# Rotating queries and keys in the layout they are multiplied in, without turning them first

## The reference

```python
qkv = x @ w_qkv (+ bias in the first attention)
q: 32 heads of 16, k and v: 8 heads of 16
rot = concatenate([-x2, x1])           # x1, x2: the two halves of a head
q, k = q * cos + rot * sin, k * cos + rot * sin   # cos, sin depend on the token
scores = softmax(q @ k.T * scale, masked to keys <= query)
out = (scores @ v) @ w_dense
```

## Time and profile before

| | us |
|---|---|
| median of 3 runs (lowest, highest) | 2409.13 (2407.0, 2411.66) |
| profiled execution: its time, its span | 2416.49, 2414.8 |
| PE busy (share of the span) | 2254.6 (93%) |
| VectorE busy | 1464.6 (61%) |
| ScalarE busy | 1183.2 (49%) |
| GpSimd busy | 506.3 (21%) |
| mean granted clock of TensorE | 0.963 |

### The profile page before, as it was taken

The page is one execution under the profiler, slowest core; times in us unless marked ns, Lnnn a source line. Parts: engine busy times, 40 slices in busy tenths (PEclk is TensorE's granted clock), DMA queues, the critical chain, the costliest instruction groups (busy, mean ns, idle before and its releaser), DMA issues.

```text
span 2414.8 us, 36047 instructions
## 1 busy us (share of the span) xinstructions
PE 2254.6 (93%) x12664; PEld 1220.6 (51%) x12664; DVE 1464.6 (61%) x3257; ACT 1183.2 (49%) x2273; POOL 506.3 (21%) x646
## 2 busy tenths in 40 slices
PE   6688898999999999999899999989898999999998
PEld 5455554545455455555555555545443444444443
DVE  6767787857667576787877778777752221221222
ACT  5465677645556465565666666576861101011010
POOL 4433323212312122131312222122220000000000
PEclk8699898999999999999999999999999999999999
DMA  5000324312313123231413133243323000000000
GB/s 179 1 1 19 104 82 164 103 47 72 117 42 114 35 58 120 80 108 53 144 53 112 54 106 116 78 122 98 100 61 97 0 18 0 14 5 5 13 1 18
DMA packets 135122, 163.59 MB, mean 68 GB/s; under 512 B 41616, under 2 KB 96912, under 8 KB 134672
## 3 DMA queue, kind: packets, MB, share of 16 engines
q1 hardware_dynamic: 134944, 161.29, 21.7%
HBM read 94.51 MB, written 53.35 MB: 61 GB/s over the span
## 4 chain that ended last, share of the span: by engine, by line
PE 76%; DMA 6%; DVE 6%; ACT 4%; SPq 3%; issue 2%; POOL 1%; ACTq 0%; POOLq 0%; DVEq 0%
PE ps L1505 15%; PE ps L1443 10%; PE ps L1516 7%; PE ps L1413 7%; PE ps L1397 7%; PE ps L1422 5%; PE ps L1458 5%; PE ps L1367 3%; PE ps L1286 3%; DMA scr_q<-big 3%; PE ps L1372 3%; PE ps L1467 2%; PE ps L1490 2%; PE ps L1378 1%; DVE peaks L2086 1%
## 5 line engine op out<-in xcount | busy, mean ns | idle before, releaser
L2086 DVE TENSOR_REDUCE peaks<-ps 128x4 f32<-128x512 f32 x960 | 625.0, 681 | 220.3 <-PE ps L1367 91.3
L1697 ACT ACTIVATE big<-ps 128x512 f32<-128x512 f32 x960 | 551.5, 603 | 362.7 <-PE ps L1397 252.9
L1901 POOL TENSOR_SCALAR_AFFINE_SELECT big<-big 128x512 f32<-128x512 f32 x384 | 248.3, 660 | 1010.6 <-ACT big L1697 1010.2
L1505 PE MATMUL ps<-xt,big 128*128 128x512 f32 x896 | 390.1, 593 | 2.8 <-issue 2.8
L1397 PE MATMUL ps<-big 99*128 99x512 bf16 (+3 forms) x1536 | 347.5, 305 | 23.5 <-ACT big L1697 18.2
L1443 PE MATMUL ps<-big,xt 128*128 128x512 f32 (+1 forms) x768 | 295.7, 497 | 0.5 <-DVE peaks L2086 0.2
L1505 PEld LDWEIGHTS ps<-xt,big 128*128 128x128 f32 x896 | 168.8, 190 | 209.3 <-issue 208.2
L1413 PE MATMUL ps<-big,vs 128*32 128x512 f32 (+3 forms) x3072 | 247.7, 450 | 11.5 <-POOL big L1901 8.2
L1786 ACT ACTIVATE t<-ps 128x512 f32<-128x512 f32 x56 | 33.5, 598 | 457.6 <-PE ps L1505 457.6
L1686 ACT ACTIVATE ps<-cbf 128x512 f32<-128x512 bf16 x384 | 230.8, 605 | 37.3 <-DVE peaks L2086 31.5
L2142 DVE SCALAR_TENSOR_TENSOR t<-rest,t 128x512 f32<-128x512 f32 x56 | 38.7, 691 | 280.4 <-PE ps L1505 276.8
(11 more groups left out here) (225 smaller groups left out, 2906.2 us busy)
## 6 DMA issues: line engine op xcount, KB each, us to landing
big<-scr_q SPq DMA_DIRECT2D x96, 384.0 KB, 4.1
scr_q<-big SPq DMA_DIRECT2D x48, 384.0 KB, 2.9
scr_q<-big SPq DMA_DIRECT2D x48, 256.0 KB, 3.1
recb<-scr_sums SPq DMA_DIRECT2D x96, 128.0 KB
big<-scr_k SPq DMA_DIRECT2D x48, 192.0 KB, 3.3
big<-in_ffn_gu SPq DMA_DIRECT2D x14, 512.0 KB, 6.2
scr_q<-big SPq DMA_DIRECT2D x48, 128.0 KB, 3.2
ctxt<-ots SPq DMA_DIRECT2D x192, 32.0 KB
```

What stands on the lines that cost most here:

```text
L1505: mm = pe.matmul(bank_of(kind, n, m), wgu[:, m // 2, c, way, m % 2 * P:(m % 2 + 1) * P], xt[:, c, :], start=(c == 0), stop=(c == DC - 1))
L1697: act.activation(probs[:, i * S:(i + 1) * S], bank_of("exp", g, i), ACT.Exp, scale=1.0 / 16 if attn_of(n) == 1 else 0.25).then_inc(made["p ...
L1901: pool.affine_select(block_, block_, [[0, GQ], [1, P]], ALU.is_ge, zero, base=0, channel_multiplier=-1).then_inc(made["cut"], 1)
L2086: dve.tensor_reduce(to, blocks, AX.X, ALU.max, negate=True).then_inc(made["negmax"], 1)
```

## The change

The projection of queries and keys is made with the weights as the stationary operand, so that a bank holds 128 columns of the projection by 512 tokens: chunk `c` of round `n`, in four matmuls of 512 columns. ScalarE copies the two halves of the bank crosswise into `r` (`swap`; the bias is added there in attention 1), VectorE multiplies the bank by the cosines into `t1` (`cosines`), and `rotate` multiplies `r` by signed sines and adds `t1`. `first_part` and `first_rest` read `r` in place of a bank, and there is no `turn_chunk`. The values have a unit of their own (`vproj`): sixteen matmuls of 128 columns into one bank, moved to `vs` by one instruction. The tables of cosines and sines must lie with columns of the projection on partitions, so PE turns `ropet` (`turn_tables`, item `tabs`) and ScalarE copies it out in four instructions (`rotations`), for attention 1 and, from a second load, for attention 2 and 3. All chunks of round n+1 now stand in the list ahead of the dense product of round n-1, where they stood among its blocks. The bias of queries and keys arrives as a 128x5 tile by an added, non-contiguous load. `t1`, `t2`, `a`, `r` and the bias tiles get smaller. Waits on `chunk_full` elsewhere become waits on `rest`. The diff, cut to its core:

```diff
-FRONT = ("inx", "inh", "th", "hm", "f", "hd")
+FRONT = ("tabs", "inx", "inh", "th", "hm", "f", "hd")
...
@@ -101,12 +101,10 @@
     if after < NIT:
         first += prepared(after)
     if before >= 0:
-        first = first[:-len(CHUNKS)] if after < NIT else []
-        rest = [[(0.45, ("chunk", after, c))] for c in CHUNKS] if after < NIT else [[]] * len(CHUNKS)
         for j in range(TJ):
             first += [(0.86, ("dense", before, j, c)) for c in range(DC)]
-            first += [(0, ("y", "d", before, j))] + rest[j]
-        first += [(0, ("ln", "d", before))] + rest[TJ]
+            first += [(0, ("y", "d", before, j))]
+        first += [(0, ("ln", "d", before))]
     spread(14 if n == NIT - 1 else 1, 46, first)
     if n == 0:
         spread(50, 66, [(0.5, item) for item in four_bit(2)])
...
+    items += [("tabs", 1), ("load_rope", 2)]
...
@@ -160,16 +159,11 @@
 
 def prepared(n):
     items = [(0.45, ("xt", "a", n, c)) for c in range(DC)]
-    late = []
-    for j in range(TJ):
-        for half in range(2):
-            for c in range(DC):
-                items.append((0.86 if half == 0 else 0.43, ("proj", n, j, half, c)))
-                if late and c % 2:
-                    items.append((0, late.pop(0)))
-            items.append((0, ("fill", n, j, half)))
-        late = [("rope", n, j, 0), ("rope", n, j, 1)]
-    return items + [(0, i) for i in late] + [(0.45, ("chunk", n, c)) for c in CHUNKS]
+    for nth, c in enumerate(CHUNKS):
+        if nth == 2:
+            items += [(0.9, ("vproj", n, j)) for j in range(TJ)] + [(0, ("vals", n))]
+        items += [(0.86, ("proj", n, c, k)) for k in range(DC)] + [(0, ("chunk", n, c))]
+    return items
 
 
...
         return [("PE", kind, k, columns(512, 1.68))]
     if kind == "proj":
-        return [("PE", kind, k, columns((512, 256)[k[2]], 1.68))]
+        return [("PE", "proj", k, columns(512, 1.68))]
+    if kind == "vproj":
+        return [("PE", "vproj", k, 920)]
+    if kind == "tabs":
+        return [("PE", "tabs", k, TURN), ("ACT", "rotations", k, 2500)]
...
-        return [("DVE", "added", k, 730) if attn_of(k[0]) == 1 else ("ACT", "filled", k, 660)]
-    if kind == "rope":
-        return [("DVE", ("turned", "rope")[k[2]], k[:2], (1900, 1050)[k[2]])]
+    if kind == "vals":
+        return [("DVE", "vadded", k, 750) if attn_of(k[0]) == 1 else ("ACT", "vfilled", k, 660)]
     if kind == "chunk":
-        return [("PE", "chunk", k, TURN), ("ACT", "hi", k, ROWS_ACT), ("DVE", "rest", k, ROWS_DVE),
+        return [("ACT", "swap", k, 1250), ("DVE", "cosine", k, 730), ("DVE", "rope", k, 1450), ("ACT", "hi", k, ROWS_ACT), ("DVE", "rest", k, ROWS_DVE),
                 ("ACT", "mid", k, 660), ("POOL", "lo", k, 1250), ("SP", "cw", k, 2000)]
...
+    if name == "tabs":
+        return [("load_rope", k)]
+    if name == "rotations":
+        return [("tabs_full", k)] + ([("rope", (NB - 1, CHUNKS[-1]))] if n == 2 else [])
...
+        late = [("y_full", ("f", n - 3, TJ - 1))] if k[1] == CHUNKS[1] and n >= 3 and attn_of(n - 3) < 3 else []
+        return [("proj_full", k)] + ([("rest", (n - 1, k[1]))] if n else []) + late
+    if name == "cosine":
+        before = chunk_before(n, k[1])
+        return [("proj_full", k), ("swap", k), ("rotations", (min(attn_of(n), 2),)), ("rope", before) if before else ("begin", ())]
     if name == "rope":
-        late = []
...
-        return [("rope", (NB - 1, TJ - 1))]
+        return [("tabs_full", (1,))]
...
-        if kind == "rope" and item[1:] == (3, TJ - 1, 1):
-            plan.append(("load_rope", 2))
+        if kind == "chunk" and item[1:] == (3, CHUNKS[-1]):
+            plan.append(("tabs", 2))
...
-        a = sb("a", [P, QK], F32)
-        t1 = sb("t1", [P, QK], F32)
-        t2 = sb("t2", [P, QK], F32)
-        r = sb("r", [P, TJ, QK], F32)
-        flat_r = r[:].rearrange("p j n -> p (j n)")
...
+                 (bias_v[:], ins["attn1_bqkv"][:, QK:QKV].broadcast_to((P, P))))
+            sp.dma_start(bias_c[:], ins["attn1_bqkv"][:, 0:QK].rearrange("o (c p) -> p (o c)", p=P),
+                         allow_slow_non_contiguous=True).then_inc(weights["attn1"], 16)
             sp.dma_start(t1[:, 0:3 * P], ins["masks"]).then_inc(constants, 16)
             flow_loads()
...
-                               start=(c == 0), stop=(c == DC - 1))
-                if c == DC - 1:
+                    bank_for("proj", n, c)
+                mm = pe.matmul(bank_of("proj", n, c), wp[:, k, c * P:(c + 1) * P], xt[:, k, :], start=(k == 0), stop=(k == DC - 1))
+                if k == DC - 1:
                     mm.then_inc(made["proj_full"], 1)
 
-            def turn_chunk(n, c):
-                pe.wait_ge(made["rope"], counted("rope", n, TJ - 1))
-                bank = bank_for("chunk", n, c)
-                turn_tiles(bank, lambda j: r[:, j, c * P:(c + 1) * P]).then_inc(made["chunk_full"], 1)
+            def project_values(n, j):
+                if j == 0:
+                    pe.wait_ge(made["xt"], counted("xt", "a", n, DC - 1))
+                    pe.wait_ge(proj_in, 16 * attn_of(n))
+                    bank_for("vproj", n)
+                for k in range(DC):
+                    mm = pe.matmul(bank_of("vproj", n)[:, j * P:(j + 1) * P], xt[:, k, j * P:(j + 1) * P], wp[:, k, QK:QKV],
+                                   start=(j == 0 and k == 0), stop=(k == DC - 1), skip_group_check=True)
+                if j == TJ - 1:
+                    mm.then_inc(made["vproj_full"], 1)
+            def turn_tables(A):
+                pe.wait_ge(rope_in, 16 * A)
+                bank = bank_for("tabs", A)
+                turn_tiles(bank, lambda j: ropet[:, j].rearrange("p w k -> p (w k)")).then_inc(made["tabs_full"], 1)
...
+            def rotations(A):
+                act.wait_ge(made["tabs_full"], counted("tabs_full", A))
+                if A == 2:
+                    act.wait_ge(made["rope"], counted("rope", NB - 1, CHUNKS[-1]))
+                bank = bank_of("tabs", A)
+                act.activation(cs[0:64, 0, :], bank[0:64], ACT.Copy)
+                act.activation(cs[64:P, 0, :], bank[0:64], ACT.Copy)
+                act.activation(cs[0:64, 1, :], bank[64:P], ACT.Copy, scale=-1.0)
+                act.activation(cs[64:P, 1, :], bank[64:P], ACT.Copy).then_inc(made["rotations"], 1)
+            def swap(n, c):
+                act.wait_ge(made["proj_full"], counted("proj_full", n, c))
+                if n:
+                    act.wait_ge(made["rest"], counted("rest", n - 1, c))
+                if c == CHUNKS[1] and n >= 3 and attn_of(n - 3) < 3:
+                    act.wait_ge(made["y_full"], counted("y_full", "f", n - 3, TJ - 1))
+                if n == 0 and c == CHUNKS[0]:
+                    act.wait_ge(weights["attn1"], 48)
+                bank = bank_of("proj", n, c)
+                if attn_of(n) == 1:
+                    act.activation(r[0:64, c, :], bank[64:P], ACT.Identity, bias=bias_c[64:P, c:c + 1])
+                    act.activation(r[64:P, c, :], bank[0:64], ACT.Identity, bias=bias_c[0:64, c:c + 1]).then_inc(made["swap"], 1)
                     return
-                if j == 0:
-                    act.wait_ge(made["pv_full"], counted("pv_full", 8 * (n - 2) + 7, 1))
-                act.activation(a[:, 512:QK], bank[:, 0:P], ACT.Copy)
-                act.activation(vs[:, n % 2, j, :, 0:HD], bank[:, P:2 * P].rearrange("p (h d) -> p h d", h=NKV),
-                               ACT.Copy).then_inc(made["filled"], 1)
...
                 slot = flow.slot[n, c]
-                act.wait_ge(made["chunk_full"], counted("chunk_full", n, c))
+                act.wait_ge(made["rope"], counted("rope", n, c))
                 if flow.written_by[n, c] > 1:
                     act.wait_ge(parts_out[slot], 48 * (flow.written_by[n, c] - 1))
-                act.activation(qp[:, slot, 0, :], bank_of("chunk", n, c), ACT.Copy).then_inc(made["hi"], 1)
+                act.activation(qp[:, slot, 0, :], r[:, c, :], ACT.Copy).then_inc(made["hi"], 1)
 
             def second_part(n, c):
...
+            def cosines(n, c):
+                dve.wait_ge(made["proj_full"], counted("proj_full", n, c))
+                dve.wait_ge(made["swap"], counted("swap", n, c))
+                dve.wait_ge(made["rotations"], counted("rotations", min(attn_of(n), 2)))
+                before = chunk_before(n, c)
+                if before:
+                    dve.wait_ge(made["rope"], counted("rope", *before))
                 else:
                     dve.wait_ge(made["begin"], counted("begin"))
-                dve.wait_ge(rope_in, 16 if attn_of(n) == 1 else 32)
-                cos = ropet[:, j, 0, :].unsqueeze(1).broadcast_to((P, 2 * CH, 64))
-                sin = ropet[:, j, 1, :].unsqueeze(1).broadcast_to((P, CH, 64))
-                ah = a[:].rearrange("p (c w k) -> p c w k", w=2, k=64)
-                th = t2[:].rearrange("p (c w k) -> p c w k", w=2, k=64)
```

(60 more changed lines are left out.)

135 lines of the change are left out of this document (56 added, 79 removed).

## The result

The changed kernel took 2425.98 us, the median of four runs (2423.69 to 2428.36), against 2408.65 us (2407.0 to 2411.66) for the kernel before beside it. The ratio is 1.0071 with a 95% interval of [1.0053, 1.0088]: 17.3 us slower. The forecast was 2415 (2387 to 2438), 6 us slower: the sign and the largest cause were right, and the result lies inside the range, but the change cost nearly three times what was forecast.

What follows compares the result with a forecast made beforehand. PE was taken as the bound from about 400 us, the chain from x's load before. -24.2 + 1.5 + 3 + 36 + 6 - 10 - 6 = +6.3 gave 2422.8 us profiled, 2415 in the median, range 2387 to 2438.

Steps and rivals of the forecast that it cites:

- Tables first in PE's order: At the start, PE waits for both tables and turns x at about 44 us, not 7.99: +36 us (30 to 40).
- One bank less: The second table holds its PSUM bank until round 3's last chunk, about 620 us: +6 us (0 to 26).
- Turned chunks: In rounds 1 to 11, PE no longer turns 55 chunks of r at 0.44 us each: -24.2 us.
- ScalarE and the longer path: ScalarE gets 40 us more work and chunks cross between ScalarE and VectorE six times: +3 us (-4 to +10).
- VectorE: Per round it loses some 11.4 us and gets 10.2, three operations a chunk at about 0.68 us each.
- Start and burst: Earlier first maxima, some 25 us after the first projection: -10 us; round 1's chunks one by one, not bursting: -6.
- values: The values' matmuls become short, 32 passes of 128 columns a round: +1.5 us (0 to 2.7).
- The signs of error: Wrong if x turns at 8 us, first exponents make up over 35 us, or rounds 1 to 8 don't shorten.
- A: The forecast itself, all terms as summed: 2415 us, own range 2403 to 2427; chance 0.50.
- D: The held bank and the chunks' longer way cost much more, 26 + 10: 2442 us, half-way 2430; chance 0.18.
- B: Early keys fill all PE loses at the start (20), the burst goes (14), bank only 2: 2393 us; chance 0.24.
- C: The tables don't stop PE, as x stands ahead or the table lands early: 2375 us; chance 0.08.

Runs made afterwards that it cites:

- the square: Four medians against before: upper row, first table early: second early +17.3, second late +2.8; lower row, first late: -14.0 and -28.6 us.
- E5: The kernel before with one added wait, so that PE doesn't start until the rotation table is in: 2440.19 us, ratio 1.0129.
- E2: The changed kernel with the first table modelled as landing at 60 us, so PE turns x first; second table's bank still held: 2392.37 us, ratio 0.9943.
- E3: The changed kernel with the first table modelled at 60 us and the second turned only after round 3's last chunk: 2377.79 us, ratio 0.9876.
- E6: The kernel before with each chunk of r turned twice into the same bank, 240 more transposes: 2430.28 us, ratio 1.0098.
- E10: E3 with one ScalarE copy of 128 partitions a chunk in place of two of 64, halves not swapped; second timing: 2374.45 us, ratio 0.9845.
- E11: E3 with two more ScalarE copies of 64 partitions in each chunk, four in all: 2404.49 us, ratio 0.9981.
- E9: The same kernel as E3, timed again: 2374.63 us, ratio 0.9857 to the kernel before.
- E4: E3 with the first table's modelled landing at 45 us in place of 60: 2374.1 us, ratio 0.9872.

## Why the prediction was right in sign and short in size

Along the square the 17.3 us are -28.6 for the change without the tables, +31.4 for the first table, +4 for the second one's load (x at 42.9 against 38.9) and +10.5 for what is left of the second; that they add up is by construction. The forecast had -35.7, +36 and +6. Its first two nearly cancel, so the sign that it gave hung on the 6 us of the bank alone: it was right by a margin smaller than the error of single terms. By its steps:

- **Tables first in PE's order** (+36): right. The order came out as forecast, and the first table landed at 38.1 us against 37.9; the second took 2.6 us to land, not 4.0, so x came at 42.85 against "about 44", and the first projection at 245 against "about 243". Measured were 31.4 and 4, and 33.8 for 30.8 in E5. One reading was wrong without consequence: the 3.66 us of sixteen transposes at the start were put to "the lower clock", but the trace gives a granted clock of 1.00 for 8 to 12 us (last section).
- **One bank less** (+6, up to 26): the term that was sized too low. "I take 6" stands against 10.5 us in the square's upper row and 14.6 in the lower. The interval of either row alone reaches down to about 5 us and so doesn't exclude the 6; that both rows lie above it, and that PE's waits grow alike in both, speaks for more. The bounds held. The one row of before that the step could name was that the trace "shows no wait put down to it", which speaks for nothing: as E2 beside E3 shows, a missing bank appears as waits on other engines. The place was right in part: its upper bound came from 250 to 300 us, and the traces of E2 and E3 part by 7.9 us before 207 us and by the rest between 207 and 420 us.
- **Turned chunks** (-24.2): right. E6 gives 0.42 us a chunk, and rounds 3 to 11 together are 23.9 us shorter than before's, 2.7 each, and 20.3 shorter than E5's, 2.3 each, against "some 2.2". Round by round that is uneven: round 3 gained 5.5 us (147.4 to 141.9), round 4 nothing (145.0 to 145.2).
- **ScalarE and the longer path** (+3, -4 to +10): not contradicted. The second copy is worth between 0 and 8 us by two timings. The upper end for one copy was right: 64 partitions by 512 took 684 ns with a bias and 128 partitions 687 (E10). ScalarE's busy time rose by 58.6 us in all, not 40. `first_part`, which now reads SBUF, took 626 ns on average against 600 from a bank, close to the 33 ns more that the prediction took from its rows. How near the load is to a limit is open: E11 says only that two copies more are too many.
- **VectorE**: the guess of 0.68 us an operation holds for the cosine product (0.69 without a bias, 0.74 with one); the two that work on `r` took 0.80 on average, with the long ones all beside GpSimd (last section). It made no difference, as PE stayed the bound in the rounds.
- **Start and burst** (-10, -6): less certain. With E3's -28.6, less turns, values and 4 for the path, -10 is left; with E9's -35.3, -17. The first maxima came 31.7 us after the first projection in E3, 32.0 in the kernel after, against 42.5 before and "some 25" in the forecast. Here the step can be named: 25 is 42.3 less 20.7 plus 3.4, the wait for the key chunk alone, while the first maxima need a query chunk too (6.9 by the prediction's own figures, so 28.5). The first exponents of E3 were only 5.4 us earlier than before, though its first maxima were 10.7 earlier. That no stretch like 350 to 385 us would come back was wrong for the kernel after (12.6 us lost at 420 to 455 us, 14.6 before) and half right for E3 (6.1 us at 385 to 420 us, where E2 with the bank held loses 11.8). By these traces the bank and the burst are not independent terms, as the sum took them to be.
- **The signs of error** named in advance: PE did not turn x at 8 us, the projection's lateness was not made up at the first exponents but grew, and round 3 and after did get shorter.

So the miss of 11 us is 4.5 for the bank (8.6 by the lower row), -0.6 for the tables and 7.1 for a smaller gain of the change itself. The last is about as large as the difference between the two timings of the same kernel (28.6 and 35.3), so its parts stay open; that the second table costs over 10 us beyond its load is what the medians of both rows of the square say. The result is inside A's own range (2403 to 2427). D, which had the bank and the way of a chunk cost more, was at 2430 half-way; the result lies between it and the forecast. B's earlier keys did not fill the start. C's price for a change without the wait was 34 us under before; E3, E4 and E9 measured 28.6, 31.0 and 35.3 under.

Not tried: freeing the bank by copying the second table out at once into a tile of its own, which needs another 4 KB of SBUF in each partition.

## What to carry to other kernels

When a new item may be scheduled freely, work out where the planner puts it against each assumed arrival time: an operand that is "there at 0" in the model but lands at 38 us stops an engine that follows its order strictly, and in this kernel, where nothing overtakes the chain of the start, the stop passed whole to the end. Ask of every added item how long it keeps its buffer, and price a held PSUM bank by the idle time of the stretch where banks are fewest, even if no wait names it. A saving off the busiest engine (0.42 us a chunk) is real but small beside one misplaced wait; moving two lines of dependencies turned 17 us slower into about 30 faster.

## What the runs showed of the hardware that was not expected

ScalarE takes as long for 64 partitions as for 128, 684 against 687 ns with a bias and 593 against 595 without.

VectorE's products and sums on `r`, with all operands in SBUF, have two kinds of durations: the median of the 60 at L2291 is 684 ns, as for the cosine product from a bank (690), but the mean is 802 and the longest 1561. VectorE and then GpSimd of the kernel after in order of time:

```profile
258.63 1.55 DVE L2291 TENSOR_TENSOR r<-r,cs 128x512 f32<-128x512 f32 x1
260.22 0.69 DVE L2292 TENSOR_TENSOR r<-r,t 128x512 f32<-128x512 f32 x1
...
745.17 0.68 DVE L2291 TENSOR_TENSOR r<-r,cs 128x512 f32<-128x512 f32 x1
745.88 1.00 DVE L2292 TENSOR_TENSOR r<-r,t 128x512 f32<-128x512 f32 x1
```

```profile
258.48 1.16 POOL L1941 TENSOR_TENSOR big<-rest,big 128x512 bf16<-128x512 f32 x1 [5.62 <-ACT big L1780]
...
745.21 2.17 POOL L1948 TENSOR_SCALAR_AFFINE_SELECT big<-big 128x512 f32<-128x512 f32 x2 [5.46 <-ACT big L1721]
```

The long ones lie beside a GpSimd instruction. In this trace 47 of the 180 operations of L2291, L2292 and L2300, which all read two operands in SBUF, took over 720 ns, and all 47 overlap one; of the 100 that overlap none, not one did. The trace of E3 has 49 and again none of 100. The one of 1.55 us began beside a product on GpSimd that ran from 258.48 to 259.64, and the one that starts right behind it takes 0.69. Not every meeting is dear: the one at 745.17 us took 0.68 beside GpSimd, the next 1.00. Reading a bank this was not seen: the cosine product without a bias never took more than 693 ns, although 15 of its 40 overlap GpSimd. That reading `r` in place of a bank brought `rest` from 676 to 750 ns on average fits it. No experiment took GpSimd's work away, so a contention with GpSimd is argued from two traces, not shown.

What added copies on ScalarE cost is not linear: from one to two a chunk 0 to 8 us, from two to four 30.

TensorE's speed in the first us differs between executions of one kernel, at a granted clock of 1.00 each time (8 to 25 us). The same products in E3 and in E9, which are the same kernel:

```profile
12.27 7.06 PE L1313 MATMUL ps<-wf,xt 128*128 128x64 f32 x32 [0.78 <-ACT xt L1611]
```

```profile
12.45 3.76 PE L1313 MATMUL ps<-wf,xt 128*128 128x64 f32 x32 [0.78 <-ACT xt L1611]
```

The sixteen transposes in front of them took 3.65 us in both. E3's first projection came at 207.4 us and E9's at 200.4. So up to 7 us between two traces at that mark need no cause in the kernel; before, E2 and E3 all have the slow kind of start. What decides it, no run shows.
